# Layer 2 of a four-layer graph network: row maxima of unstacked scores on TensorE row blocks, a mask added in 32x32 blocks, and normalisation on GpSimd

## The chip, the cores and the metric

The kernel runs on one core of a Trainium2 chip. The metric is device time in microseconds (us), from the first to the last instruction and what the runtime adds around them. The kernel before takes 1164.12 us (median of three runs, 1162.89 to 1165.49).

## The reference

Four layers run one after the other over `x` (16 batches, 512 nodes, 128 features) with one 512x512 adjacency matrix `adj`; each ends in a residual and a layer norm. The change touches layer 2, masked attention with 4 heads of 32 features:

```python
qkv = h @ W                                   # (16, 512, 384)
q, k, v = ...                                 # each (16, 4 heads, 512, 32)
mask = jnp.where(adj == 0, -jnp.inf, 0.0)
scores = jnp.einsum('bhid,bhjd->bhij', q, k) / np.sqrt(HEAD_DIM) + mask
attn = jax.nn.softmax(scores, axis=-1)
out = jnp.einsum('bhij,bhjd->bhid', attn, v)
x = _layernorm(x + out, axis=-1)
```

Everything is float32 at the interface. The kernel keeps that precision by splitting operands into a high part that TensorE multiplies in one pass (float32r) and a low part that holds the rest.

## The kernel before, in words

`build` runs `layer0_setup`, `layer0`, `layer1`, `layer2` and `layer3` in turn; each has a block in which every engine has its own instruction list, tied together by semaphores. `x` stays in SBUF as `m.X`. `mask_ij` and `mask_ji` hold -1e30 where an edge is missing, with rows i or rows j on the partitions.

Layer 2 is a software pipeline over the 16 batches. In step s every engine runs through the list `ORDER`; the item `what` works on batch s - STAGE[what]. The helper `pairs` unrolls the first steps, loops over two steps at a time and unrolls the last ones. `Fori` is the hardware loop. A step of the full pipeline holds, for one batch each:

- `N T R B Y`: batch norm of layer 1 applied (ScalarE), turned (TensorE, L1282), added to the residual (VectorE, L1197), statistics (VectorE), 1/sqrt (GpSimd, L505 and L507), applied (VectorE, L513) and copied into `m.X` (GpSimd, L1117).
- `x q k v`: the batch is turned (L1287), split in two parts, and multiplied with the weights: q and k in three float32r passes (L58 to L60), v in float32 (L1299). q and k are split in two again as `qkT`.
- stacking: SyncE copies `qkT` by DMA into `qk_st` (L1088), so that one head has 96 rows: high, high, low of q against high, low, high of k. A product over 96 rows then has all three terms. Row 96 takes the negated row maximum of q's side against a row of ones.
- `s`, 16 of them (4 heads by 4 row tiles): one product of 96 rows (L1306) into a PSUM bank; VectorE adds `mask_ij` and takes the maximum along the row in one instruction (L1221, and a second that reads the accumulator).
- `g n`: the 16 maxima are negated, turned (L1310), copied out (L1164) and sent by DMA into row 96 (L1079).
- `t`, 8 of them (4 heads by 2 pairs of column tiles): the transposed scores (L1319) and `mask_ji` through an identity matrix (L1320), two banks (`wide`, 128x1024) each; ScalarE takes the exponential of both (L1160).
- `a`, 4 of them: output and denominator (L1331). Each is four matmuls that use 32 columns of the array each and fill 32 partitions of bank 4 or 5, over four steps of j. They are float32, which the trace shows as two records per matmul.
- `e o d m r b y`: copied out (L1168, L1170), turned back (L1338, L1343), divided (L1231, L1237), residual (L1243), layer norm (statistics on VectorE, L492 and L498; root on GpSimd; application on VectorE, L513).

Items in `RING` take banks 6 and 7 in turn, and before TensorE writes into one it waits for what the item before last released (`wait_for_bank`): for an `s` that is its maximum on VectorE. So two units of scores can be in flight.

Of the kernel before, what the change touches and what calls it, by code (L numbers as in the profile page):

```python
# [20 lines left out]
F32 = mybir.dt.float32  # L21
# [6 lines left out]
P = 128  # L28
B, N, D = 16, 512, 128
NT = N // P  # L30
# [36 lines left out]
def setup_constants(nc, ctx, m, ins, bank):  # L67
# [9 lines left out]
    m.mask_ji = sb("mask_ji", [P, NT, N], BF16)  # L77
    m.AhT = [sb("AhT_hi", [P, NT, N], F32R), sb("AhT_lo", [P, NT, N], F32R)]
# [888 lines left out]
def layer2(nc, m, ins, bank, wide):  # L967

    SCALE = float(HD) ** -0.5
    JP = NT // 2
    PAIRS = H * JP
    TILES = H * NT
    with ExitStack() as own:
# [3 lines left out]
        def sem(name):  # L992
# [7 lines left out]
        xTr = [[sb(f"xT{k}{h}", [P, N], F32R) for h in range(2)] for k in range(2)]  # L1000
        qkT = [sb(f"qkT{k}", [P, 4, N], F32R) for k in range(2)]
        Q_LO, Q_HI, K_HI, K_LO = range(4)
        qk_st = [sb(f"qk_st{k}", [P, 2, H, N], F32R) for k in range(2)]
        q_st = [s[:, 0] for s in qk_st]
        k_st = [s[:, 1] for s in qk_st]
        v = [sb(f"v{k}", [P, NT, D]) for k in range(2)]
        junk = [sb(f"junk{k}", [P, N], BF16) for k in range(2)]
        mx = [sb(f"mx{k}", [P, TILES]) for k in range(2)]
        neg = [sb(f"neg{k}", [P, TILES]) for k in range(2)]
        neg_row = [sb(f"neg_row{k}", [TILES, P], F32R) for k in range(2)]  # L1010
        prob = [[sb(f"prob{k}{h}", [P, 2, N]) for h in range(H)] for k in range(JP)]
# [9 lines left out]

        w_in = sem("w_in"); w_hi = sem("w_high"); w_lo = sem("w_low"); const = sem("const")
        x_f = sem("x_in_place")
# [4 lines left out]
        stacked = [[sem(f"stacked{k}{h}") for h in range(H)] for k in range(2)]  # L1028
        s_ps = sem("scores"); s_mx = sem("row_max")
        n_sb = sem("negated"); n_ps = sem("neg_turned"); n_row = sem("neg_row_out")  # L1030
        row_in = [sem(f"row_in{k}") for k in range(2)]
        t_ps = sem("scores_t"); t_exp = sem("exp_done")
        av = sem("values")
# [4 lines left out]
        psO, psD = bank[4], bank[5]  # L1038
# [10 lines left out]
        ORDER = []  # L1049
        for what in ("s s g Y a n s N R x T a B s q k a s e s a s s t s t s d t m o r s t t s v b t s s y t t s s").split():  # L1050
            ORDER.append((what, sum(w == what for w, _ in ORDER)))

        RING = [item for item in ORDER if item[0] in "Txqkvsnod"]
        ring = {item: bank[6 + n % 2] for n, item in enumerate(RING)}

        def released(s, what, k):

            b = s - STAGE[what]
            return {"x": (x_c, after(b, 1)), "q": (q_lo, after(b, 1)), "k": (k_lo, after(b, 1)),
                    "v": (v_c, after(b, 1)), "s": (s_mx, after(b, TILES, k + 1)),  # L1060
                    "n": (n_row, after(b, 1)), "o": (o_n, after(b, 1)),
                    "d": (rcp, after(b, 1)), "T": (res1, after(b, 1))}[what]

        def of_batch(what, s, par, nth):

            back = STAGE[what]
            return s - back, (par + back) % 2, nth + (par - back) // 2

        @block.sync
        def _(sp):  # L1070
            sp.dma_start(W[:], ins["L2_gnn_W"]).then_inc(w_in, 16)
            for k in range(2):
                sp.sem_inc(row_in[k], 16)

            def step(s, par, alive, nth):
                if alive[2]:
                    sp.wait_ge(n_row, after(s - 2, 1))
                    hold(sp, gate)
                    sp.dma_start(q_st[par][3 * HD:3 * HD + 1].bitcast(F32).rearrange("a h (t p) -> a (h t) p", p=P),  # L1079
                                 neg_row[par][:].bitcast(F32)).then_inc(row_in[par], 16)  # L1080
                if alive[0]:
                    sp.wait_ge(k_lo, after(s, 1))
                    for h in range(H):
                        sp.wait_ge(t_ps, after(s - 2, PAIRS, (h + 1) * JP))
                        if h == 0:
                            hold(sp, gate)
# [596 lines left out]
```

## Time and profile before

| | |
|---|---|
| median of 3 runs | 1164.12 us |
| the profiled execution, span | 1163.7 us |
| steps of layer 2 with all stages full | 12, from 592 to 914 us |
| layer 2 in all | from 500 to 983 us |
| TensorE busy over the span | 86% |
| VectorE, ScalarE, GpSimd busy | 63%, 39%, 17% |

The profile comes from one profiled execution, whose span is 1163.7 us; this lies 0.4 us under the median of the runs, so one can be read for the other. "Busy" of an engine is the union of its instruction records. Matmul records overlap, since each begins before the one ahead of it has left the array: what one costs in a stream is read from start to start. "PEld" is the loading of the stationary operand. In the names, `128*32` means that the stationary operand has 128 rows and 32 columns. "Granted clock" is a share of 2.4 GHz; 0.5 is 1.2 GHz.

### The profile page before, as it was taken

Reading aid. Unit: us, or ns where it says so; the run is one execution under the profiler, and the core shown is the slowest. Engines: PE = TensorE matmul, PEld = TensorE weight load, DVE = VectorE, ACT = ScalarE, POOL = GpSimd, SP = SyncE. Lnnn points to the kernel's source line nnn. Section 1 sums busy time; section 2 is a strip of 40 time slices with the busy share of each in tenths; the row PEclk is TensorE's granted clock in tenths of the full one; section 3 lists DMA queues with packets and bytes.
Section 4 is the critical chain, followed back from the end, with each engine's and each line's share of the span. In section 5 each row is a group of like instructions: output and inputs, shape, how many; then the busy total and the mean of one; then the engine's idle time right before and its main releaser. Section 6 shows DMA issues by size and latency. Waiting matters only on the chain. (4 is left out here: it accounts for less than half of the span.)

```text
span 1163.7 us, 19102 instructions
## 1 busy us (share of the span) xinstructions
PE 1002.3 (86%) x5486; PEld 681.5 (59%) x5532; DVE 727.6 (63%) x2226; ACT 450.3 (39%) x734; POOL 198.0 (17%) x266
## 2 busy tenths in 40 slices
PE   3969999999997697926899999999999995899995
PEld 2748999999997586413444444444444442566663
DVE  7853455554454565635667767777777642688885
ACT  2111121121120265710444444544544442577762
POOL 5000110111100000050011111111111001155554
PEclk7879999999998899955799999999999998899998
DMA  6000000000000000004222222222223200000001
GB/s 185 1 28 19 10 19 19 10 18 18 9 0 1 9 0 0 0 8 108 55 56 55 54 54 54 54 58 64 66 60 68 66 1 3 1 27 27 27 27 37
DMA packets 32629, 40.07 MB, mean 34 GB/s; under 512 B 6352, under 2 KB 15696, under 8 KB 32592
## 3 DMA queue, kind: packets, MB, share of 16 engines
q1 hardware_dynamic: 32592, 39.61, 13.9%
q8 instruction: 19, 0.31, 0.1%
q14 instruction: 18, 0.15, 0.0%
HBM read 5.91 MB, written 4.19 MB: 9 GB/s over the span
## 5 line engine op out<-in xcount | busy, mean ns | idle before, releaser
L1221 DVE CUSTOM_DVE_ANT_0 junk<-bank,mask_ij 128x512 bf16<-128x512 f32 x256 | 170.7, 689 | 80.7 <-PE bank L1306 75.6
L1160 ACT ACTIVATE prob<-wide 128x1024 f32<-128x1024 f32 x128 | 128.0, 1024 | 44.5 <-PE wide L1320 44.1
L1306 PE MATMUL bank<-qk_st 96*128 96x512 f32 x256 | 122.2, 517 | 25.3 <-DVE mx L1221 15.8
L1319 PE MATMUL wide<-qk_st 128*128 128x512 f32 x256 | 116.2, 523 | 0.3 <-ACT prob L1160 0.3
L596 ACT CAST yT<-wide 128x512 fp32r<-128x512 f32 x48 | 28.1, 586 | 217.6 <-PE wide L699 162.7
L505 POOL TENSOR_SCALAR n_rstd<-n_aggr 128x4 f32<-128x4 f32 x64 | 12.6, 198 | 506.7 <-DVE n_aggr L498 494.6
L1306 PEld LDWEIGHTS bank<-qk_st 96*128 96x128 f32 x256 | 49.2, 201 | 82.5 <-DVE mx L1221 37.4
L1320 PE MATMUL wide<-mask_ji,identb 128*128 128x512 bf16 x226 | 88.8, 393 | 0.0
L58 PE MATMUL bank<-z,L3T_hi 128*128 128x256 f32 x256 | 73.8, 288 | 6.3 <-DVE z L657 6.3
L1633 PEld LDWEIGHTS bank<-Wh,pr 128*128 128x128 f32 x512 | 61.1, 196 | 23.8 <-issue 19.9
L1633 PE MATMUL bank<-Wh,pr 128*128 128x129 f32 x512 | 65.3, 282 | 10.9 <-ACT pr L1501 10.9
L60 PE MATMUL bank<-z,L3T_lo 128*128 128x256 f32 x256 | 73.8, 288 | 0.0
L59 PE MATMUL bank<-z,L3T_hi 128*128 128x256 f32 x256 | 73.6, 288 | 0.0
L1331 PE MATMUL bank<-prob,v 128*32 128x512 f32 x512 | 68.1, 604 | 1.8 <-ACT prob L1160 1.8
L507 POOL TENSOR_TENSOR n_rstd<-n_rstd,neg_half 128x4 f32<-128x4 f32 x64 | 66.3, 1036 | 5.5 <-POOL n_rstd L505 0.2
L1331 PE MATMUL bank<-prob,ones_hd 128*32 128x512 f32 x512 | 66.6, 592 | 0.0
L643 DVE TENSOR_TENSOR yT<-wide,yT 128x512 fp32r<-128x512 f32 x48 | 32.9, 686 | 50.9 <-ACT yT L596 50.9
L1320 PEld LDWEIGHTS wide<-mask_ji,identb 128*128 128x128 bf16 x256 | 24.7, 96 | 62.3 <-issue 59.2
L58 PEld LDWEIGHTS bank<-z,L3T_hi 128*128 128x128 f32 x256 | 50.3, 196 | 7.6 <-DVE z L657 6.8
L1319 PEld LDWEIGHTS wide<-qk_st 128*128 128x128 f32 x256 | 50.5, 197 | 4.0 <-ACT prob L1160 1.3
L619 POOL TENSOR_TENSOR Xr<-Xf,Xr 128x512 fp32r<-128x512 f32 x16 | 20.3, 1288 | 185.1 <-ACT Xr L591 185.1
L513 POOL TENSOR_SCALAR rc<-rc,n_aggr,n_rstd 128x128 f32<-128x128 f32 x64 | 50.0, 794 | 3.4 <-POOL n_rstd L507 3.4
(256 smaller groups left out, 2273.3 us busy)
## 6 DMA issues: line engine op xcount, KB each, us to landing
qk_st<-qkT SPq DMA_DIRECT2D x192, 128.0 KB, 2.4
Xf<-X SPq DMA_DIRECT2D x16, 256.0 KB, 2.3
out_dram<-rc SPq DMA_DIRECT2D x16, 256.0 KB, 2.3
A<-in_adj_dram SPq DMA_DIRECT2D x1, 1024.0 KB, 5.5
w<-in_L_gnn_W_dram SPq DMA_DIRECT2D x2, 128.0 KB, 2.3
qk_st<-neg_row SPq DMA_DIRECT2D x16, 8.0 KB, 1.8
W<-in_L_gnn_W_dram SPq DMA_DIRECT2D x1, 192.0 KB, 2.4
w_sb<-in_L_gnn_w_dram SPq DMA_DIRECT2D x1, 64.0 KB, 5.0
```

The lines of the kernel that those rows point to most:

```text
L58: pe.matmul(out, stat[0], mov[0], start=start, stop=False)
L59: pe.matmul(out, stat[0], mov[1], start=False, stop=False)
L60: return pe.matmul(out, stat[1], mov[0], start=False, stop=stop)
L507: pool.tensor_tensor(rstd[:], rstd[:], self.m.neg_half[:, 0:4], ALU.pow).then_inc(self.s_rstd, 1)
L513: eng.tensor_scalar(out(k), r[:, k], self.aggr[parity][:, k, 0:1], self.rstd[parity][:, k:k + 1], ALU.subtract, ALU.mult).then_inc(self.s_ ...
L1160: act.activation(flat(prob[jp][h][:]), wide[k % 2][:], ACT.Exp, scale=SCALE).then_inc(t_exp, 1)
L1221: dve.tensor_tensor_reduce(out=junk[k % 2][:], in0=src[:], in1=m.mask_ij[:, k % NT], scale=1.0, scalar=3.0 * MASKED, op0=ALU.add, op1=ALU.max,
L1306: pe.matmul(out[:], q_st[bp][0:3 * HD, h, i * P:i * P + P], k_st[bp][0:3 * HD, h], start=True, stop=True).then_inc(s_ps, 1)
L1319: pe.matmul(ps, k_st[bp][:, h, j * P:j * P + P], q_st[bp][:, h], start=True, stop=False)
L1320: last = pe.matmul(ps, m.identb[:], m.mask_ji[:, j], start=False, stop=True)
L1331: last = pe.matmul(ps[c, :], v[bp][:, k, c] if stat is None else stat[:], prob[jp][h][:, jj], start=(k == 0), stop=(k == NT - 1), skip_gro ...
L1633: last = pe.matmul(out_bank[h][:, t * (D + 2):t * (D + 2) + D + 1], pr[par][:, j, k * P:k * P + P], Wh[par][:, j, 0:D + 1], start=(j == 0) ...
```

## The change

Only `layer2` is new, beside one remembered address and the declaration of the PSUM banks (a third pair, `wide[2]`, is banks 4 and 5).

1. `s` has 8 units in place of 16. A unit is one row tile of two heads: two matmuls of 32 rows each, on neighbouring row blocks of the array, of `qkT`'s high parts alone, into banks 4 and 5; then `mask_ij` through the identity into each bank. VectorE takes one plain maximum over 2x512. There is only this one pair of banks, so a unit waits for the maximum of the unit before.
2. `t` has 4 units, one head each, over banks 0 to 3: four matmuls of `qk_st`, then `mask_ji` in 16 matmuls of 32x32 (row block j, column block c), from a rearranged copy `mask_q`, which 16 DMAs fill once.
3. `a` becomes `D` (denominators) and `V` (outputs), each a complete accumulation over j in a bank of the ring; `prob` is double buffered (two of its eight parts lie where `AhT` of layer 1 was), and `qk_st` single.
4. The maxima are turned and sent in two halves (`n`, `m`), negated by ScalarE's copy.
5. GpSimd applies both norms, copies, subtracts for `xT`'s low part, and adds the residual. VectorE has none of these.
6. Stages: 6 deep in place of 5; every engine has an order of its own.

```diff
-        STAGE = dict(N=0, T=0, R=0, B=0, Y=1, x=1, q=1, k=1, v=2, s=2, g=3, n=3, t=3,
-                     a=4, e=4, o=4, d=4, m=4, r=4, b=4, y=4)
...
+        DEPTH = 6
+        STAGE = dict(N=0, T=0, R=0, B=1, x=1, q=1, k=1, v=2, s=2, n=2, m=3, t=3, E=3,
+                     D=4, V=4, e=4, f=4, d=4, o=4, c=4, b=5)
...
+        PE_ORDER = order("t s m D D s D D t s V V x s V V t s n s q d t o s k v T s")
+        ACT_ORDER = order("E E m e E E x f E E n q N E E k v")
+        DVE_ORDER = order("B s s s b s s s q c s k R s")
+        RING = [(what, k) for what, k in PE_ORDER if what in "TxqkvnmoVDd" and (what not in "VD" or k == 0)]
         ring = {item: bank[6 + n % 2] for n, item in enumerate(RING)}
...
+                if alive[1]:
+                    b, bp = s - 1, 1 - par
+                    norm1.root(pool, b + CREDIT, bp)
+                    norm1.apply(pool, b + CREDIT, bp, Xf[bp], lambda k: Xf[bp][:, k])
+                    pool.wait_ge(norm1.s_x, after(b, 4))
+                    hold(pool, gate)
+                    pool.tensor_copy(batch_flat(m.X, b), flat(Xf[bp][:])).then_inc(x_f, 1)
+                    pool.wait_ge(x_c, after(b, 1))
+                    pool.wait_ge(k_ps, after(b - 1, 1))
+                    pool.tensor_tensor(xTr[1][:], xT[bp][:], xTr[0][:].bitcast(F32),
+                                       ALU.subtract).then_inc(x_lo, 1)
+                if alive[5]:
+                    b, bp = s - 5, 1 - par
+                    norm.root(pool, b + CREDIT, bp)
+                    norm.apply(pool, b + CREDIT, bp, r, lambda k: r[:, k])
...
-                        dve.tensor_tensor_reduce(out=junk[k % 2][:], in0=src[:], in1=m.mask_ij[:, k % NT],
-                                                 scale=1.0, scalar=3.0 * MASKED, op0=ALU.add, op1=ALU.max,
-                                                 accum_out=mx[bp][:, k:k + 1]).then_inc(s_mx, 1)
...
+                        dve.tensor_reduce(mx[bp][:, col:col + NT + 1:NT], wide[2][:].rearrange("p (h n) -> p h n", h=2),
+                                          AX.X, ALU.max).then_inc(s_mx, 1)
...
-                        pe.matmul(out[:], q_st[bp][0:3 * HD, h, i * P:i * P + P], k_st[bp][0:3 * HD, h],
-                                  start=True, stop=True).then_inc(s_ps, 1)
...
+                        pe.wait_ge(s_mx, after(b, UNITS, k))
+                        for hh in range(2):
+                            c = slice((2 * pair + hh) * HD, (2 * pair + hh + 1) * HD)
+                            pe.matmul(bank[4 + hh][:], qkT[bp][c, Q_HI, i * P:i * P + P], qkT[bp][c, K_HI],
+                                      start=True, stop=False)
+                        for hh in range(2):
+                            last = pe.matmul(bank[4 + hh][:], m.identb[:], m.mask_ij[:, i], start=False, stop=True)
+                        last.then_inc(s_ps, 1)
...
-                            pe.matmul(ps, k_st[bp][:, h, j * P:j * P + P], q_st[bp][:, h], start=True, stop=False)
-                            last = pe.matmul(ps, m.identb[:], m.mask_ji[:, j], start=False, stop=True)
...
+                        for j in range(NT):
+                            if j % 2 == 0:
+                                pe.wait_ge(t_exp, after(b, EXPS, 2 * k - 1 + j // 2))
+                            pe.matmul(bank[j][:], k_st[:, k, j * P:j * P + P], q_st[:, k], start=True, stop=True)
+                        for c in range(4):
+                            for j in range(NT):
+                                q = slice(32 * j, 32 * j + 32)
+                                last = pe.matmul(bank[j][32 * c:32 * c + 32, :], m.identb[q, q], mask_q[q, c],
+                                                 start=False, stop=True, skip_group_check=True)
                         last.then_inc(t_ps, 1)
```

How the change moves instructions. On TensorE, in the full step before, the stretch from the last two `a` items on. `bank<-qk_st` is a unit of scores, `bank<-prob,v` and `bank<-prob,ones_hd` the two halves of an `a`, `wide<-qk_st` with `wide<-mask_ji,identb` the transposed scores:

```order
L1331 MATMUL bank<-prob,v 32x512 x4
L1331 MATMUL bank<-prob,ones_hd 32x512 x4
L1306 MATMUL bank<-qk_st 128x512 x2
L1331 MATMUL bank<-prob,v 32x512 x4
L1331 MATMUL bank<-prob,ones_hd 32x512 x4
...
L1306 MATMUL bank<-qk_st 128x512
...
L1306 MATMUL bank<-qk_st 128x512
...
L1319 MATMUL wide<-qk_st 128x512
L1320 MATMUL wide<-mask_ji,identb 128x512
L1319 MATMUL wide<-qk_st 128x512
L1320 MATMUL wide<-mask_ji,identb 128x512
```

The beginning of a full step of the change. `wide<-qk_st` with the 16 rows of `mask_q` is one `t`; `wide<-qkT` with `wide<-mask_ij` is one `s`; `ident,mx` is the turned maximum:

```order
L1340 MATMUL wide<-qk_st 128x512 x4
L1344 MATMUL wide<-mask_q,identb 32x512 x16
L1322 MATMUL wide<-qkT 128x512 x2
L1325 MATMUL wide<-mask_ij,identb 128x512 x2
L1282 MATMUL bank<-ident,mx 8x128
L1355 MATMUL bank<-prob,ones_hd 32x512 x8
L1322 MATMUL wide<-qkT 128x512 x2
L1325 MATMUL wide<-mask_ij,identb 128x512 x2
L1355 MATMUL bank<-prob,ones_hd 32x512 x8
L1340 MATMUL wide<-qk_st 128x512 x4
L1344 MATMUL wide<-mask_q,identb 32x512 x16
```

Each `s` and each `t` now has matmuls of two shapes, 32-row or 32x32 blocks beside whole ones, where before only the `a` items had blocks. Later in the same step, in the stretch from the third `t` on, two units of scores stand next to each other with only the turned maximum between them; the product of q and the turned denominators (`ident,denT`) follow:

```order
L1340 MATMUL wide<-qk_st 128x512 x4
L1344 MATMUL wide<-mask_q,identb 32x512 x16
L1322 MATMUL wide<-qkT 128x512 x2
L1325 MATMUL wide<-mask_ij,identb 128x512 x2
L1282 MATMUL bank<-ident,mx 8x128
L1322 MATMUL wide<-qkT 128x512 x2
L1325 MATMUL wide<-mask_ij,identb 128x512 x2
L58 MATMUL bank<-xT_hi,Wr 128x512
L59 MATMUL bank<-xT_lo,Wr 128x512
L60 MATMUL bank<-xT_hi,Wr 128x512
L1366 MATMUL bank<-ident,denT 128x128 x4
```

Before, the units of one step were spread between `a` items and in groups of two or three over two banks; here each has the one pair of banks to itself.

On GpSimd a full step before had two roots and one copy. Now, in the last unrolled step ahead of the loop (n1 is the norm of layer 1, n2 that of layer 2), it has:

```order
L506 TENSOR_SCALAR n_rstd<-n_aggr 128x4 [waits n1_aggr,n1_x]
L508 TENSOR_TENSOR n_rstd<-n_rstd,neg_half 128x4 [waits n1_eps]
L514 TENSOR_SCALAR Xb<-Xb,n_aggr,n_rstd 128x128 [waits n1_rstd]
L514 TENSOR_SCALAR Xb<-Xb,n_aggr,n_rstd 128x128 x3
L1116 COPY X<-Xb 128x512 [waits n1_x]
L1119 TENSOR_TENSOR xT_lo<-xT,xT_hi 128x512 [waits k_in_psum,xT_out]
L506 TENSOR_SCALAR n_rstd<-n_aggr 128x4 [waits n2_aggr,n2_x]
L508 TENSOR_TENSOR n_rstd<-n_rstd,neg_half 128x4 [waits n2_eps]
L514 TENSOR_SCALAR rb<-rb,n_aggr,n_rstd 128x128 [waits n2_rstd]
L514 TENSOR_SCALAR rb<-rb,n_aggr,n_rstd 128x128 x3
L1127 COPY X<-rb 128x512 [waits n2_x]
L1133 TENSOR_TENSOR rb<-rb,X 128x512 [waits out_divided,x_in_place]
```

The chain from the statistics to the turned batch (`x`) now passes through four GpSimd instructions where VectorE had them.

## Rows read from the trace of the kernel before

**Rows 1.** Timeline of ScalarE: start, length, instruction, idle before and releaser
```profile
591.99 0.59 ACT L1168 COPY oT<-bank 128x512 f32<-128x512 f32 x1 [3.81 <-PE bank L1331]
914.30 0.59 ACT L1168 COPY oT<-bank 128x512 f32<-128x512 f32 x1 [3.81 <-PE bank L1331]
```
**Rows 2.** Busy time by stretch: stretch, engines busy with counts, PEclk, DMA share, GB/s
```profile
619.04:914.30 295.26, 273.89 (x1548) 125.26 (x1571) 211.01 (x695) 141.40 (x187) 31.90 (x53) 1.00 0.27 59
500.20:591.99 91.79, 59.12 (x212) 30.05 (x214) 47.70 (x153) 22.40 (x33) 18.93 (x20) 0.65 0.24 54
```
**Rows 3.** Waits of TensorE from 619.04 to 914.30: total us, times, longest
```profile
PE bank L1306 <- DVE mx L1221: 10.0, 11, 1.0
```
**Rows 4.** Timeline of TensorE, pieces of one full step
```profile
731.13 0.60 PE L1338 MATMUL bank<-ident,oT 128*128 128x128 f32 x4
731.49 0.48 PE L1306 MATMUL bank<-qk_st 96*128 96x512 f32 x1
...
732.07 0.58 PE L1319 MATMUL wide<-qk_st 128*128 128x512 f32 x1
...
732.53 0.58 PE L1319 MATMUL wide<-qk_st 128*128 128x512 f32 x1
...
733.96 1.16 PE L1299 MATMUL bank<-W,xT 128*128 128x128 f32 x8
734.87 0.48 PE L1319 MATMUL wide<-qk_st 128*128 128x512 f32 x1
735.19 0.39 PE L1320 MATMUL wide<-mask_ji,identb 128*128 128x512 bf16 x1
...
749.06 0.40 PE L60 MATMUL bank<-xT,Wr 128*128 128x512 f32 x1
749.39 1.06 PE L1331 MATMUL bank<-prob,v 128*32 128x512 f32 x8
750.27 1.04 PE L1331 MATMUL bank<-prob,ones_hd 128*32 128x512 f32 x8
751.24 0.72 PE L1306 MATMUL bank<-qk_st 96*128 96x512 f32 x2
751.90 1.06 PE L1331 MATMUL bank<-prob,v 128*32 128x512 f32 x8
```
**Rows 5.** Timeline of TensorE in layer 3: whole float32 matmuls, two records each
```profile
1060.16 1.02 PE L1624 MATMUL wide<-xTc,wB 128*128 128x512 f32 x2
1061.01 1.02 PE L1627 MATMUL wide<-xTc,wB 128*128 128x512 f32 x2
```
**Rows 6.** One line alone, the plain reduction of 2048: min/median/max ns
```profile
L296 DVE TENSOR_REDUCE deg<-A x1: 2286/2286/2286, 34.6 to 34.6; 128x4 f32<-128x2048 f32 x1
```
**Rows 7.** Instruction groups, 619.04 to 914.30: count | busy us, mean ns | idle before
```profile
L1221 DVE CUSTOM_DVE_ANT_0 junk<-bank,mask_ij 128x512 bf16<-128x512 f32 x176 | 117.1, 689 | 47.7 <-PE bank L1306 44.6 <-DVE mx L1221 3.1
```
**Rows 8.** Timeline: VectorE releases TensorE, TensorE releases ScalarE
```profile
748.35 0.08 DVE L1221 DVE_READ_ACCUMULATOR2_ANT mx<- 128x1 f32 x1
748.49 0.50 PE L58 MATMUL bank<-xT,Wr 128*128 128x512 f32 x1 [0.67 <-DVE mx L1221]
...
755.03 0.39 PE L1320 MATMUL wide<-mask_ji,identb 128*128 128x512 bf16 x1
...
755.46 1.02 ACT L1160 ACTIVATE prob<-wide 128x1024 f32<-128x1024 f32 x1 [0.49 <-PE wide L1320]
```
**Rows 9.** Groups of GpSimd over the whole span, columns as in Rows 7
```profile
L507 POOL TENSOR_TENSOR n_rstd<-n_rstd,neg_half 128x4 f32<-128x4 f32 x64 | 66.3, 1036 | 5.5 <-POOL n_rstd L505 0.2
L513 POOL TENSOR_SCALAR rc<-rc,n_aggr,n_rstd 128x128 f32<-128x128 f32 x64 | 50.0, 794 | 3.4 <-POOL n_rstd L507 3.4
L619 POOL TENSOR_TENSOR Xr<-Xf,Xr 128x512 fp32r<-128x512 f32 x16 | 20.3, 1288 | 185.1 <-ACT Xr L591 185.1
```
**Rows 10.** Timeline of GpSimd, the start of layer 2
```profile
499.88 11.08 POOL L1102 MEMSET qk_st<- 32x2048 f32 x6
```
**Rows 11.** Timeline of VectorE, the end of layer 2
```profile
981.68 1.11 DVE L513 TENSOR_SCALAR X<-rb,n_aggr,n_rstd 128x128 f32<-128x128 f32 x4 [1.66 <-POOL n_rstd L507]
```

More of the change, by code:

```diff
@@ new lines, in neg, with stack @@
+            def neg(b, p):
+                sp.wait_ge(n_row[p], after(b, 1))
+                sp.wait_ge(t_ps, after(b - 1, H, 2 * p + 2))
+                hold(sp, gate)
+                sp.dma_start(q_st[3 * HD:3 * HD + 1, 2 * p:2 * p + 2].bitcast(F32).rearrange("a h (t p) -> a (h t) p", p=P),
+                             neg_row[p][:].bitcast(F32)).then_inc(row_in[p], 16)
+            def stack(b, bp, h):
+                sp.wait_ge(t_ps, after(b - 1, H, h + 1))
+                hold(sp, gate)
+                for g, (q, k) in enumerate(((Q_HI, K_HI), (Q_HI, K_LO), (Q_LO, K_HI))):
+                    sp.dma_start(qk_st[g * HD:(g + 1) * HD, :, h].bitcast(F32),
+                                 qkT[bp][h * HD:(h + 1) * HD, q:k + 1:k - q].bitcast(F32)).then_inc(stacked[h], 16)
@@ L1075, in step @@
             def step(s, par, alive, nth):
+                if alive[3]:
+                    neg(s - 3, 1)
                 if alive[2]:
[L1077 to L1086, printed above, removed]
-                        for g, (q, k) in enumerate(((Q_HI, K_HI), (Q_HI, K_LO), (Q_LO, K_HI))):
-                            sp.dma_start(qk_st[par][g * HD:(g + 1) * HD, :, h].bitcast(F32),
-                                         qkT[par][h * HD:(h + 1) * HD, q:k + 1:k - q].bitcast(F32)
-                                         ).then_inc(stacked[par][h], 16)
+                    b = s - 2
+                    sp.wait_ge(q_lo, after(b, 1))
+                    sp.wait_ge(k_lo, after(b, 1))
+                    stack(b, par, 0)
+                    stack(b, par, 1)
+                    neg(b, 0)
+                    stack(b, par, 2)
+                    stack(b, par, 3)
@@ L1127, in step @@
             def step(s, par, alive, nth):
-                for what, k in ORDER:
+                for what, k in ACT_ORDER:
                     if not alive[STAGE[what]]:
@@ L1166, in step @@
                         act.wait_ge(av, after(b, NT))
                         act.wait_ge(o_ps, after(b - 1, 1))
[L1168 to L1172 removed]
+                        act.copy(oT[:], ring["V", 0][:]).then_inc(o_c, 1)
+            pairs(act, B, DEPTH, step)
         @block.vector
         def _(dve):
[L1176 removed]
+            for s in (res1, q_lo, k_lo, rcp, o_n):
@@ new lines, in step @@
+                        for c in range(4):
+                            for j in range(NT):
+                                q = slice(32 * j, 32 * j + 32)
+                                last = pe.matmul(bank[j][32 * c:32 * c + 32, :], m.identb[q, q], mask_q[q, c],
+                                                 start=False, stop=True, skip_group_check=True)
+                        last.then_inc(t_ps, 1)
+                    elif what in "DV":
+                        acc = ring[what, 0]
+                        if what == "D" and k == 0:
+                            pe.wait_ge(t_exp, after(b, EXPS))
+                        if what == "V" and k == 0:
+                            pe.wait_ge(v_c, after(b, 1))
+                        for h in range(H):
+                            c = slice(h * HD, (h + 1) * HD)
+                            last = pe.matmul(acc[c, :], ones[:] if what == "D" else v[bp][:, k, c], prob[bp][h][:, k],
+                                             start=(k == 0), stop=(k == NT - 1), skip_group_check=True)
+                        last.then_inc(dn if what == "D" else av, 1)
```

260 lines of the change are left out of this document (122 added, 138 removed).

## The prediction

> **What bounds the kernel now.** I read how long a step is first, then the busy time by stretch, the waits and the timeline of TensorE. In the twelve full steps of layer 2, which run from 591.99 to 914.30 us by ScalarE's copy of the output, one per step [rows 1], a step takes (914.30 - 591.99) / 12 = 26.86 us. Over eleven of them TensorE is busy 273.89 of 295.26 us, VectorE 211.01, ScalarE 141.40, GpSimd 31.90, at the full clock [rows 2]. So TensorE sets the step: idle (295.26 - 273.89) / 11 = 1.94 us per step. Of that, 10.0 / 11 = 0.9 us is a unit of scores that waits for the maximum two before it on VectorE [rows 3]. VectorE has 211 / 11 = 19.2 us of work and is late only there.
>
> From start to start on the timeline of TensorE [rows 4]: a pair `t` matmul and mask matmul 732.53 - 732.07 = 0.46 us, so 0.23 for one full matmul; a half of an `a` 0.88. A step before is then
>
> - `s`: 16 x 0.23 = 3.7
> - `t`: 16 x 0.46 = 7.4
> - `a`: 4 x 1.96 = 7.8 (0.88, then 0.97 with the way out, then 0.11 more in what follows, below)
> - idle 1.9
> - what is left of 26.86: 6.0, for q, k, v, five turnings and small gaps. This part stays.
>
> **The change on TensorE.** Three prices aren't in the trace as such.
>
> *Change of shape.* The `a` items use 32-column blocks and stand between whole matmuls. L60 to L1331 takes 749.39 - 749.06 = 0.33 in place of 0.23; the second half of the `a` takes 751.24 - 750.27 = 0.97 in place of 0.88; and the two L1306 behind it take 0.66 in place of 0.46, which holds the 0.11 of the way out and 0.10 of the next way in [rows 4]. A way in and out is thus 0.10 + 0.09 + 0.11 = 0.30 us. Not all of it is the shape: the matmul behind v's product, which has no blocks, also takes 735.19 - 734.87 = 0.32. So the shape itself costs 0.2. The bounds for the round trip in a new item are 0 (everything hidden) and 0.30; I take 0.20. The Trainium skill ("TensorEngine Tiling (Array Packing)", Key Properties) says that a change of tiling mode drains TensorE. The trace agrees with that for column blocks, by 0.2 to 0.3 us; for row blocks no row here shows it. That rule speaks against this change, which makes 12 such round trips more in each step. By a drain of nothing the sum would be about 2 us less per step.
>
> *Two row blocks at once.* The two 32-row matmuls of an `s` cost 0.23 if they run side by side, 0.46 if not. The nearest row is the `a`: its half has four float32 matmuls (eight records) in 0.88 us [rows 4], and one whole float32 matmul of 512 columns in layer 3 takes 1061.01 - 1060.16 = 0.85 [rows 5]: four column blocks run at once. I take 0.23 for the pair. An `s` is then 0.23 + 2 masks x 0.23 + 0.20 = 0.89, and 8 x 0.89 = 7.1.
>
> *Sixteen 32x32 blocks.* All at once 0.23, four at once as the `a` does 4 x 0.23 = 0.92. I take 0.25, since rows and columns of blocks are separate here and banks too. `t` is 4 x 0.23 + 0.25 + 0.20 = 1.37, and 4 x 1.37 = 5.5. The Trainium skill ("TensorE: Matmul & The Clock Gate", Measured speedup vs the span model) gives 10.6 times for sixteen such tiles. By that the mask would be 0.23 x 16 / 10.6 = 0.35 us, an estimate from the page, and the step 0.4 us longer.
>
> `D` and `V` have as many matmuls as `a`: 7.8. At four places (`D s`, and `t s` three times) one block shape follows another, so a way is saved: -0.4. One more turned maximum: +0.2.
>
> **The new waits on TensorE.** An `s` waits for the maximum of the `s` ahead. The plain maximum over 2x512 is half of 2286 ns, 1.15 us [rows 6], as against two of 0.69 [rows 7]. From VectorE's end (748.35 + 0.08) to TensorE is 0.06; from the slot of the last matmul (755.03 + 0.23) to the reader is 0.20 [rows 8]. So `s` to `s` needs 0.20 + 1.15 + 0.06 = 1.4 us of other work between them. Six of the eight gaps have 1.8 us or more. Between the fifth and sixth there is only the turned maximum, 0.15: a wait of 1.3 us. Behind it on TensorE are q, d and the fourth `t`, and all that is left of the step.
>
> The second wait is `T`, in the bank of k. The low part of k on VectorE comes after k's copy on ScalarE, which stands behind the two exponentials of the fourth `t`: 0.20 + 2 x 1.02 + 0.59 + 0.69 (ScalarE and VectorE as in [rows 1, 7, 8]) and some 0.1 of handing over are 3.6 us after that `t`. TensorE has o, `s`, k and v meanwhile: 0.36 + 0.89 + 3 x 0.23 + 0.91 [rows 4] = 2.85. So 0.8 us. I see no third one above 0.1: idle 1.3 + 0.8 + 0.1 = 2.2.
>
> Sum of a step: 7.1 + 5.5 + 7.8 - 0.4 + 0.2 + 6.0 + 2.2 = 28.4 us, 1.55 more than 26.86. What TensorE is spared in `t` (1.9) it more than pays in `s` (3.4), since the mask left VectorE for it.
>
> **The other engines** don't set the step. VectorE: 8 x 1.15 for 16 x 0.69, and about 4.4 us of norm application, residual and subtraction gone: near 15 us. GpSimd: two roots 2 x 1.3, two applications 2 x 4 x 0.79, a subtraction and an addition 2 x 1.29 [rows 9], copies 1.2: 12.7 us in 28. Its chain from the statistics to `x` is 1.4 + 1.3 + 3.2 = 6 us from the start of the step, and TensorE comes to `x` at 11. These edits cost nothing while that is so; without the 5 us of cover a slower GpSimd would go one to one into the step. The DMAs: `qk_st` is single, but a head's stack is copied as soon as its `t` is done and is wanted a step later; the copy takes some 2 us. The maxima of heads 0 and 1 leave at 18 us of the step and are wanted at its end. The 16 DMAs for the mask are issued before the first `t` by over 50 us.
>
> **Start and end.** The six memsets of 11.08 us hold up the first statistics and root [rows 10]; three are left: -5.5. At the end a residual on GpSimd (1.3 for 0.7), the application (3.2 for 1.1 [rows 11]), and a copy (0.6): +3.3. Together -2. The steps that fill and drain (91.8 us ahead of the first full one, at 0.65 of the clock [rows 2]) have the same items; I count four of them, half each, so 14 steps: 14 x 1.55 = 22.
>
> 1163.7 + 22 - 2 = 1183.7 us; the median shown is 0.4 above the profiled span, so **1184**.
>
> **Rivals.**
>
> 1. *Faster.* The change of shape costs nothing where the next stationary operand can be loaded meanwhile: 8 x 0.2 + 4 x 0.2 - 0.4 = 2.0 less, 26.4 per step: 1163.7 - 14 x 0.46 - 2 = 1155. If the waits also fall into gaps that I count under the 6.0, it reaches 1125. For it: VectorE is relieved by 4 us, and the waits of before (0.9 and others) go. Against it: the 0.30 around each `a`, and the fixed 1.3.
> 2. *Slower, the blocks don't run at once.* Row blocks one after another: 8 x 0.23 = 1.8 more per step, 1184 + 14 x 1.8 = 1209. If the mask also goes four by four, 0.67 x 4 = 2.7 more, 1247. Against: the `a`. For: there the blocks are columns only. This is also the case in which the change doesn't do what it says.
> 3. *Slower, TensorE is bound by issue.* The densest stretch in the rows is an `a`: 16 instructions, loads included, in 0.88 us, 55 ns each. If that were a limit, 32 instructions for a mask take 1.76 in place of 0.25: 6.0 more per step, 1268. It decides as soon as the queue is used up; 1.76 us of mask behind 8 instructions of `t` would do that. The same 0.88 is explained by the columns alone, so the trace doesn't tell. The Trainium skill ("TensorE: Matmul & The Clock Gate", Wait — 56ns, not 53.3ns?) names about 62 ns per matmul where instructions are decoded in software, and about 25 where not.
>
> **How the numbers follow.** Forecast 0.42 (its own range 1168 to 1206, from the round trip between 0.15 and 0.30 and the mask up to 0.5); rival 1 0.36; rival 2 0.14; rival 3 0.08. The 0.36 is high because three terms that I added (change of shape, both waits) are worked out, not seen, and all on the same side. The range is 1128 to 1235: it leaves out the far ends of rivals 1 and 2 and all of rival 3. A measurement here tells 0.2% (2.3 us) from nothing: faster 0.36, same 0.05, slower 0.59.
>
> **What would show it.** A step of 28.4 us between ScalarE's copies; `s` about 0.89 from the first matmul to what follows, `t` 1.4; a wait of TensorE of 1.3 us per step for the maximum, ahead of the sixth `s`, and one of 0.8 ahead of L1295; VectorE near 15 us per step; GpSimd near 12.7 and not waited for. The prediction is wrong in its size if the two row matmuls start 0.23 apart, if the sixteen start over more than 0.5 us, and in its sign if whole matmuls follow blocks 0.23 later.

## The result, and the profile after

| | before | after |
|---|---|---|
| median | 1164.59 us (1162.89 to 1165.49) | 1169.34 us (1168.72 to 1169.67) |
| profiled span | 1163.7 | 1166.9 |
| forecast | | 1184 (1128 to 1235) |

The change is slower by 0.44%: ratio 1.0044, interval 1.0029 to 1.0058. The side was the one forecast, the size was not: +4.8 us where I had +20.

First the length of a step. From one reciprocal of the denominators on VectorE to the next it is 26.93 us before (mean of eleven) and 27.44 after: +0.51, where 1.55 was forecast. The busy times of the twelve-step stretch (columns: stretch, PE, PEld, DVE, ACT, POOL, PEclk, DMA share, GB/s) are, after,

```profile
592.00:907.00 315.00, 288.81 (x2360) 131.76 (x2393) 173.40 (x336) 146.01 (x206) 142.92 (x183) 1.00 0.26 59
```

VectorE has 173.40 x 27.44 / 315 = 15.1 us per step (19.2 before [rows 2]), GpSimd 12.5. Both were forecast (15 and 12.7). TensorE still sets the step, at the full clock. Its waits from 620 to 900 us, in the order total, times, longest:

```profile
PE wide L1322 <- DVE mx L1239: 12.1, 10, 1.2
PE bank L1295 <- DVE qkT L1231: 6.4, 11, 0.6
PE wide L1325 <- issue: 4.9, 31, 0.2
```

The wait of [rows 3] is gone, and the first two stand where the prediction put them: 1.21 us ahead of the sixth unit of scores (forecast 1.3), 0.58 ahead of L1295 (forecast 0.8). The third line is gaps of 0.16 us inside a unit, between its pair and its mask; they are counted as part of `s` below. The timeline of TensorE after, in pieces:

```profile
706.32 0.65 PE L1295 MATMUL bank<-ident,on 128*128 128x128 f32 x4 [0.58 <-DVE qkT L1231]
706.90 0.50 PE L1322 MATMUL wide<-qkT 32*128 32x512 f32 x2
707.34 0.61 PE L1325 MATMUL wide<-mask_ij,identb 128*128 128x512 bf16 x2
707.59 1.28 PE L1340 MATMUL wide<-qk_st 128*128 128x512 f32 x4
708.80 0.43 PE L1344 MATMUL wide<-mask_q,identb 32*32 32x512 bf16 x16
709.26 0.50 PE L1322 MATMUL wide<-qkT 32*128 32x512 f32 x2
...
725.11 0.27 PE L1282 MATMUL bank<-ident,mx 128*8 128x128 f32 x1
726.59 0.50 PE L1322 MATMUL wide<-qkT 32*128 32x512 f32 x2 [1.21 <-DVE mx L1239]
```

These answer to [rows 4]. Read the starts. The pair of row blocks has 707.34 - 706.90 = 0.44 us until the next item: 0.23 for two at once and 0.21 for the way out of the shape. Four `t` matmuls have 708.80 - 707.59 = 1.21, and the sixteen blocks 709.26 - 708.80 = 0.46 (0.36 in the step's other three). The sixteen start within 0.05 us of one another. So all sixteen run beside each other, and the two row blocks too; `e4` to `e6` below test both. The other rows:

```profile
L1239 DVE TENSOR_REDUCE mx<-wide 128x2 f32<-128x1024 f32 x128 | 156.8, 1225 | 163.2 <-PE wide L1325 162.1
L508 POOL TENSOR_TENSOR n_rstd<-n_rstd,neg_half 128x4 f32<-128x4 f32 x64 | 67.0, 1046 | 5.5 <-POOL n_rstd L506 0.2
```

The plain maximum of 2x512 takes 1.23 us (1.15 forecast from [rows 6]), in place of two of 0.69 [rows 7]. The root is as in [rows 9]. In the full steps no wait of TensorE names GpSimd.

At the ends, the memsets fell from 11.08 us [rows 10] to 5.55, and the first root starts at 509.56 in place of 512.69. The last item of layer 2 ends at 986.58, before at 982.79. These 3.8 us are the sum of four parts: the first reciprocal comes 3.7 earlier, the eleven full steps take 5.6 more, the last four between reciprocals 1.7 less, and from the last reciprocal to the end it is 3.6 more.

### The profile page after: what moved, and what is told of

It is laid out like the page before. It is cut to its first block and busy times, and to the rows that moved or that the text cites. A ratio compares the mean times of both kernels' runs of the same rounds, so it can differ in the third digit from the quotient of the medians.

```text
span 1166.9 us, 20377 instructions
## 1 busy us (share of the span) xinstructions
PE 999.8 (86%) x6510; PEld 678.1 (58%) x6572; DVE 657.4 (56%) x1666; ACT 447.9 (38%) x750; POOL 345.3 (30%) x439
## 5 line engine op out<-in xcount | busy, mean ns | idle before, releaser
L1239 DVE TENSOR_REDUCE mx<-wide 128x2 f32<-128x1024 f32 x128 | 156.8, 1225 | 163.2 <-PE wide L1325 162.1
L1322 PE MATMUL wide<-qkT 32*128 32x512 f32 x256 | 66.1, 511 | 26.8 <-DVE mx L1239 25.9
L1340 PE MATMUL wide<-qk_st 128*128 128x512 f32 x256 | 78.5, 428 | 0.8 <-ACT prob L1182 0.7
L1325 PE MATMUL wide<-mask_ij,identb 128*128 128x512 bf16 x210 | 70.3, 400 | 7.5 <-issue 7.5
L652 DVE TENSOR_TENSOR G<-wide,bias_field 128x384 f32<-128x384 f32 x64 | 35.7, 558 | 71.0 <-PE wide L60 71.0
L58 PE MATMUL wide<-Pj_hi,yT 128*128 128x384 f32 x192 | 64.5, 336 | 2.8 <-DVE yT L644 2.8
L1322 PEld LDWEIGHTS wide<-qkT 32*128 32x128 f32 x256 | 24.5, 187 | 69.6 <-DVE mx L1239 53.7
L60 PE MATMUL wide<-Pj_hi,yT 128*128 128x384 f32 x192 | 64.3, 335 | 0.0
L59 PE MATMUL wide<-Pj_lo,yT 128*128 128x384 f32 x192 | 64.3, 335 | 0.0
L514 POOL TENSOR_SCALAR rb<-rb,n_aggr,n_rstd 128x128 f32<-128x128 f32 x64 | 50.3, 799 | 3.4 <-POOL n_rstd L508 3.4
L514 POOL TENSOR_SCALAR Xb<-Xb,n_aggr,n_rstd 128x128 f32<-128x128 f32 x64 | 50.3, 798 | 3.4 <-POOL n_rstd L508 3.4
```

Of the source, the lines that this page charges most:

```text
L58: pe.matmul(out, stat[0], mov[0], start=start, stop=False)
L59: pe.matmul(out, stat[0], mov[1], start=False, stop=False)
L60: return pe.matmul(out, stat[1], mov[0], start=False, stop=stop)
L514: eng.tensor_scalar(out(k), r[:, k], self.aggr[parity][:, k, 0:1], self.rstd[parity][:, k:k + 1], ALU.subtract, ALU.mult).then_inc(self.s_ ...
L1239: dve.tensor_reduce(mx[bp][:, col:col + NT + 1:NT], wide[2][:].rearrange("p (h n) -> p h n", h=2), AX.X, ALU.max).then_inc(s_mx, 1)
L1322: pe.matmul(bank[4 + hh][:], qkT[bp][c, Q_HI, i * P:i * P + P], qkT[bp][c, K_HI], start=True, stop=False)
```

## The experiments

Each is timed in turn with the kernel before on the same chip; ratios are to it, with a 95% interval. "Step" is the mean of eleven steps from reciprocal to reciprocal. Ledgers of a step are differences of starts on TensorE's timeline, waits taken out. Where the clock fell in some steps, the length of the others is given as "step at clock 1.00".

### The two waits

Theory: they cost what they last, since TensorE sets the step. `e1` moves the second half's items between the two units of scores, `e2` puts `T` behind the last unit, `e3` does both.

```diff
-        PE_ORDER = order("... V V t s n s q d t o s k v T s")
+        PE_ORDER = order("... V V t s n q d s t o s k v s T")   # e1: "n q d s", e2: "s T"
-        DVE_ORDER = order("B s s s b s s s q c s k R s")
+        DVE_ORDER = order("B s s s b s s q s c s k s R")             # e1: "q s c", e2: "s R"
```

> The changed kernel with q and the turned denominators put between the fifth and sixth unit of scores (TensorE: 's n q d s t o'; VectorE: 's q s c'). Theory A, the step is TensorE's list of work plus the waits seen on it: the wait of 1.21 us ahead of the sixth unit goes, since n, q and d take 0.27 + 0.88 + 0.36 = 1.5 us; a step 26.25 in place of 27.46, over some 14 steps -17 us, about 1152. Rival B, the wait only moves: q's low part on VectorE now comes later or the turned output waits for its bank, and the time stays within 4 us of 1169.

> The changed kernel with the turning of the next batch (T) behind the last unit of scores of the step, on TensorE ('k v s T') and VectorE ('k s R'). Theory A: the wait of 0.58 us for k's low part is covered by the unit of scores, -0.6 per step, -8 us, about 1161. Rival B: the residual R now comes right ahead of the next step's statistics and the turned maximum waits for T's bank, so the wait moves into the next step and the time stays within 3 us of 1169.

> Both moves together. Theory A: the two gains add, 25.65 us per step and about 1144 (-25). Rival B: with TensorE's idle time gone VectorE or the exponentials of ScalarE are late somewhere; more than a third of the sum is lost, over 1152.

Measured: e1 1159.35 us, 0.9965 [0.9951, 0.9978], step 26.85. e2 1160.93, 0.9971 [0.9961, 0.998], step 27.09. e3 1146.78, 0.9859 [0.9839, 0.9879], step 26.01. e1 missed by 7 us, and its waits (620 to 900 us) tell why:

```profile
PE bank L1295 <- DVE qkT L1231: 6.4, 11, 0.6
PE wide L1325 <- issue: 4.9, 31, 0.2
PE bank L1366 <- ACT neg_row L1146: 4.6, 10, 0.5
```

The wait of 1.21 is gone, and 0.47 of it comes back in the third line: `d` now comes earlier, and its bank is that of the turned maximum, whose copy stands behind two exponentials on ScalarE. At the full clock the two gains nearly add up: a step is 26.85 in e1 (-0.59), 26.53 in e2 (-0.91, more than the 0.58 of its wait) and 26.01 in e3 (-1.43). In time they don't: 10.0 and 8.4 us against 22.6 for both. The clock fell in several steps of e2 and not in those of e1 and e3 (more on this below), so that e2's mean step is 27.09. Two placements are thus worth 22.6 us, five times what the change costs, and either alone is enough to make it faster than the kernel before.

### The prices of the new shapes

`e5` puts both heads' matmuls on one row block, so that they can't run at once. `e6` reads all 128 rows in them, so no shape changes, and none run at once. `e4` adds the mask of `t` with four whole matmuls. `e12` is that edit on e3's order. e5 and e6 compute other scores than the reference.

```diff
-                            c = slice((2 * pair + hh) * HD, (2 * pair + hh + 1) * HD)
+                            c = slice(2 * pair * HD, (2 * pair + 1) * HD)      # e5
+                            c = slice(0, P)                                    # e6
...
-                        for c in range(4):
-                            for j in range(NT):
-                                q = slice(32 * j, 32 * j + 32)
-                                last = pe.matmul(bank[j][32 * c:32 * c + 32, :], m.identb[q, q], mask_q[q, c], ...)
+                        for j in range(NT):                                    # e4, e12
+                            last = pe.matmul(bank[j][:], m.identb[:], m.mask_ji[:, j], ...)
```

> The changed kernel with both 32-row matmuls of a unit of scores on the same row block (the same head twice, so the row maximum of the odd heads is that of their neighbour; everything else as it is). Theory A: what was one slot of 0.23 becomes two, +0.22 per unit, +1.8 per step, +25 us, about 1194: that is what running on two row blocks at once is worth. Rival B: they didn't run at once before (the modelled ends hide it), no change.

> The changed kernel with both matmuls of a unit over all 128 rows (the row maxima are then of the sum over the four heads; everything else as it is). No change of shape is left in a unit, and nothing runs at once: 4 x 0.22 = 0.88 us. Theory A, a change of shape in and out costs 0.2 beside the pair's 0.23: against 0.88 for a unit now, no difference per unit, within 4 us of 1169, and about 25 us under the run with one row block. Rival B, the shape costs nothing: as slow as the run with one row block.

> The changed kernel with the mask of the transposed scores added as in the kernel before: four whole matmuls with the identity per head in place of sixteen 32x32 ones. Theory A, the sixteen run at once: the trace has 0.36 us for them from their first to the next item, four whole ones take 4 x 0.22 = 0.88, so +0.45 per head less a change of shape (0.1), +1.3 to +1.8 per step, 1187 to 1195. Rival B, the sixteen with their sixteen loads cost as much as whole ones once the ways in and out are counted: within 3 us of 1169.

> The order of e3_both (1146.8 us, 26.0 us per step, longest wait 0.6 us) with t's mask as four whole matmuls instead of sixteen blocks. At full clock that edit cost 1.8 us per step in e4_mask_whole; there the steps in which TensorE's granted clock fell behind the 1.21 us wait of the sixth unit of scores were 3.5 us longer. Theory A (the fall belongs to that wait): here the wait is gone, the clock stays at 1.00, a step takes 27.8 us and the kernel 1146.8 + 14 x 1.8 = 1172 us (1168 to 1175). Theory B (the fall comes with the whole-mask matmuls whatever waits stand before them): the mean step is 28.5 or more, the clock of the layer is 0.97 or below, and the time is 1180 us or more.

| | median | ratio | step at clock 1.00 | step mean |
|---|---|---|---|---|
| e5 | 1214.7 | 1.0424 [1.0398, 1.045] | 29.3 | 30.70 |
| e6 | 1174.83 | 1.0091 [1.0074, 1.0108] | 28.0 | 28.01 |
| e4 | 1203.44 | 1.0327 [1.0311, 1.0342] | 29.25 | 29.97 |
| e12 | 1176.17 | 1.0094 [1.0077, 1.0111] | 27.8 | 27.86 |

At the full clock the prices can be read from the step. e5: +1.86 = 8 x 0.23, so a second matmul on the same row block costs its whole 0.23. e6: +0.57 = 8 x 0.07, where I had expected nothing; side by side saves 0.23 of a unit and pays 0.16 of it for the change of shape (the 1.3 us between e5 and e6 are 8 x 0.16). e4: +1.8 = 4 x 0.45, and e12 the same against e3 (27.86 - 26.01 = 1.85): at 0.92 for four whole matmuls (4 x 0.23), the sixteen blocks cost 0.92 - 0.46 = 0.46 with their change of shape. I had 0.25 + 0.20. The Trainium skill ("TensorEngine Tiling (Array Packing)", Key Properties) says that a change of mode drains TensorE; the 0.16 here agrees.

In time, e4 missed by 8 us and e5 by 21 (e6 by 2, e12 by 1). For e4 and e5 the granted clock shows where (e5, same columns as above):

```profile
714.00:716.00 2.00, 1.30 (x5) 0.42 (x5) 0.77 (x1) 1.89 (x3) 2.00 (x4) 1.00 0.00 0
716.00:718.00 2.00, 1.49 (x5) 0.63 (x5) 0.46 (x1) 0.18 (x2) 1.34 (x2) 0.71 0.01 2
718.00:720.00 2.00, 2.00 (x7) 1.51 (x7) 1.23 (x1) 0.20 (x1) 0.00 (x0) 0.50 0.70 159
720.00:722.00 2.00, 2.00 (x26) 1.32 (x25) 0.85 (x2) 1.22 (x3) 0.00 (x0) 0.94 0.19 38
...
811.00:840.00 29.00, 26.70 (x206) 12.16 (x208) 15.04 (x29) 12.75 (x18) 12.28 (x16) 1.00 0.24 55
```

```profile
715.03 0.27 PE L1282 MATMUL bank<-ident,mx 128*8 128x128 f32 x1
716.51 0.95 PE L1322 MATMUL wide<-qkT 32*128 32x512 f32 x2 [1.21 <-DVE mx L1239]
717.39 1.03 PE L1325 MATMUL wide<-mask_ij,identb 128*128 128x512 bf16 x2
717.86 0.99 PE L58 MATMUL bank<-xT_hi,Wr 128*128 128x512 f32 x1
718.65 0.63 PE L59 MATMUL bank<-xT_lo,Wr 128*128 128x512 f32 x1
719.08 0.63 PE L60 MATMUL bank<-xT_hi,Wr 128*128 128x512 f32 x1
719.50 0.97 PE L1366 MATMUL bank<-ident,denT 128*128 128x128 f32 x4
```

Behind the wait of 1.21 us the clock is 0.50 (the lower of the two levels, 1.2 GHz) for some 3 us, and a whole matmul has 719.50 - 719.08 = 0.42 instead of 0.23. In another step of the same run it stays at 1.00 (last row of the first fence). e12 tests whether the wait has to do with it. In the stretch from 592 to 907 e4 has the mean clock 0.97, and e12, with the same matmuls and a longest wait of 0.4 us, 1.00:

```profile
592.00:907.00 315.00, 305.35 (x1779) 138.67 (x1815) 172.13 (x333) 144.06 (x205) 139.54 (x179) 1.00 0.26 57
```

So the whole masks don't bring the fall by themselves. The long wait is not enough for it either, since e6 has the same one at 1.00 throughout the stretch.

### What the row mask costs

`e7` leaves the mask out of the row maxima; `e8` brings both norm applications back to VectorE (stages and orders, credits moved with them).

```diff
-                        for hh in range(2):                                    # e7
-                            last = pe.matmul(bank[4 + hh][:], m.identb[:], m.mask_ij[:, i], start=False, stop=True)
...
-        DVE_ORDER = order("B s s s b s s s q c s k R s")                       # e8
+        DVE_ORDER = order("B s s Y s b s s s q y c s k R s")
```

> The changed kernel without the two mask matmuls of a unit (the row maximum is then taken over all columns, masked ones too; the mask of the transposed scores stays). Theory A: the mask on TensorE costs 2 x 0.22 and the way out of the row shape moves into the next item, so 8 x 0.44 = 3.5 us per step; the waits for the maximum stay at 1.4 between units: the one wait grows by nothing, and a step is 27.46 - 3.5 = 24.0, 1169 - 14 x 3.5 = 1120. Rival B: VectorE's maximum then sets the pace and the gain is under half, over 1145.

> The changed kernel with both norm applications back on VectorE (as Y and y; the roots, copies, subtraction and residual stay on GpSimd). VectorE gets 2 x 1.1 us more per step. Theory A: VectorE isn't on TensorE's way while it is under 20 us in 27, and the instructions lie in its idle time: within 3 us of 1169. Rival B: every VectorE instruction ahead of a maximum delays a unit of scores, since there is one pair of banks only: +1.1 or +2.2 per step, 1184 to 1200.

e7: 1116.87 us, 0.9589 [0.9573, 0.9605], step 24.17 (24.05 but for one step). The mask costs 27.44 - 24.05 = 3.4 us of a step, 8 x 0.42, and 52.5 us in all. That is more than the whole difference of the two kernels. e8: 1172.64, 1.0077 [1.006, 1.0095], +3.3 us, just over the 3 expected; the clock is 0.98 in its mean and a new wait of 0.2 us shows in five steps. The move of the norms to GpSimd is thus worth 3.3 us at most by itself, and part of that is the clock.

### A better version

`e9` adds the row mask in 64x64 blocks, four per bank pair, as `t` does with 32x32; `e10` is e9 on e3's order; `e11` adds one move on ScalarE, against the wait that e1 brought up. Not shown: `mask_x`, a copy of the mask with its halves exchanged, which two DMAs fill once, and the two `neg_row`, which lie in one tensor.

```diff
-                        for hh in range(2):
-                            last = pe.matmul(bank[4 + hh][:], m.identb[:], m.mask_ij[:, i], start=False, stop=True)
+                        for c in range(2):
+                            for hh in range(2):
+                                q = slice(64 * hh, 64 * hh + 64)
+                                last = pe.matmul(bank[4 + hh][64 * c:64 * c + 64, :], m.identb[q, q],
+                                                 (m.mask_ij if c == hh else mask_x)[q, i], ...)
...
-        ACT_ORDER = order("E E m e E E x f E E n q N E E k v")
+        ACT_ORDER = order("E E m e E E x f E n E q N E E k v")                 # e11
```

> The changed kernel, in which the mask of a unit of scores is added in four 64x64 blocks (rows 0 to 63 for the even head's bank, 64 to 127 for the odd one's) from the mask and a copy with its halves exchanged, in place of two whole matmuls. Theory A, blocks of different rows and banks run at once, as the run with one row block showed for 32 rows: 0.22 in place of 0.44, less 0.1 for a third change of shape: -0.1 to -0.2 per unit, -1 to -1.6 per step, -14 to -22 us, 1147 to 1155. Rival B, each change of shape costs 0.1 to 0.2 with its load, and the third takes all of it back: within 4 us of 1169.

> Both moves of the order together with the mask of the scores in 64x64 blocks. Theory A: what the blocks gain alone comes on top of 1147, so 1125 to 1133. Rival B: with TensorE some 24.5 us per step the maxima on VectorE come between the units again, and at most a third of it is seen, over 1140.

> e10_all with one more move: ScalarE sends the copy of the turned maximum (n) ahead of the second exponential of its group. In e10_all and e3_both the denominator's matmuls (L1366) wait 0.47 us per step on that copy. My theory: the wait is on the path of TensorE's turn, so a step loses 0.4 to 0.5 us: 25.28 to about 24.85, 14 steps, 1138.3 - 6 = 1132 us (1130 to 1134). Rival: the wait only moves on to the next user of a bank behind it (q's copy, or the sums that wait for the exponential that is now late by the copy), and the time stays at 1137 to 1139.

e9: 1166.2 us, 1.001 [0.9999, 1.0021], step 27.34, 11 us above what was expected: its clock is 0.97 in the stretch, and each of its falls follows the wait of 1.1 us. e10: 1138.27, 0.9782 [0.9767, 0.9796], step 25.28 = 26.01 - 0.73, so 0.09 per unit, at the full clock; that is less than the 0.1 to 0.2 expected, and the time is 5 us above its range. e11: 1130.43, 0.9687 [0.9664, 0.9709], step 24.58, at the fast end of what was expected. TensorE has one wait left in the stretch, of 0.4 us:

```profile
592.00:907.00 315.00, 314.47 (x2870) 141.09 (x2869) 188.34 (x365) 161.91 (x227) 155.52 (x200) 1.00 0.29 64
```

e11 is 3.1% faster than the kernel before and 38.9 us faster than the change.

### The term that failed: a unit of scores before

The forecast gave 3.7 us of a step before to the 16 units of scores, 0.23 each. By starts they took 6.05, 0.38 each. Such a unit has 96 rows among matmuls of 128. `e13` gives it 128 rows, `e14` gives `t` 96, `e15` issues it twice, `e16` cuts it to 64 columns (all on the kernel before; the lines of e14 and e15 are not shown).

```diff
-  pe.matmul(out[:], q_st[bp][0:3 * HD, h, i * P:i * P + P], k_st[bp][0:3 * HD, h], ...)
+  pe.matmul(out[:], q_st[bp][:, h, i * P:i * P + P], k_st[bp][:, h], ...)                       # e13
+  pe.matmul(out[:, 0:64], q_st[bp][0:3 * HD, h, i * P:i * P + P], k_st[bp][0:3 * HD, h, 0:64])  # e16
```

> The kernel before with its 16 units of scores reading all 128 rows of the stack in place of 96 (the added rows hold zeros, a one and an old shift, so the maxima that they give are other numbers). Theory A: a unit takes 0.38 us and not 0.23 because its 96-row shape stands among 128-row matmuls. Then those that do not stand beside an a item (ten of 16) come down to 0.23 and the step is 1.5 to 2.4 us shorter where the wait for VectorE does not take it: 24.6 to 25.5 us, 1126 to 1141 us. Theory B: the extra does not hang on the rows: a step stays at 26.9 and the time at 1164 within 2.

> The kernel before with the 16 transposed-score matmuls on 96 rows, which leaves the subtraction of the maximum out of the exponential; their masks stay on 128 rows. Theory A (a 96-row matmul among 128-row ones pays for the change of shape): every one of the 16 now stands between masks of 128 rows and costs 0.1 to 0.2 more, the step 28.5 to 30 us, 1190 to 1215 us. Theory B (it does not hang on the rows): no change, 1164 within 2.

> The kernel before with the matmul of each unit of scores issued twice (the second overwrites the first). Theory A: a matmul costs 0.23 and the other 0.15 of a unit's 0.38 are fixed, so 16 x 0.23 = 3.7 more per step, less up to 0.9 where waits for the maximum absorb it: 29.7 to 30.6 us, 16 batches: 1209 to 1223 us. Theory B: each such matmul costs 0.38: 6.1 more per step, 33 us, 1250 us or more.

> The kernel before with the matmul of each unit of scores on 64 of its 512 columns (the maxima are then taken over 448 columns of old contents). Theory A: 448 of 512 columns are 0.20 us, so a step is 16 x 0.20 = 3.2 shorter at most, 23.7 us, and the waits for VectorE's maxima take back up to 1.5 of it: 23.7 to 25.2, 1113 to 1137 us; 0.15 per unit stay. Theory B: the unit's whole 0.38 follows the columns: 0.33 x 16 = 5.3 shorter before waits, 21.6 to 23.5 us, 1078 to 1110 us.

e13: 1164.29, 1.0003 [0.9993, 1.0012]; e14: 1164.31, 1.0 [0.9991, 1.001]. The rows are not it. e15: 1205.53, 1.0355 [1.0337, 1.0372], step 29.47, +2.54, 3.5 us under the range of its theory A and far from B. The waits in its steps fell meanwhile (620 to 900 us; the longest was 1.0 and is 0.6):

```profile
PE bank L1307 <- DVE mx L1221: 5.0, 9, 0.6
PE bank L58 <- DVE mx L1221: 3.3, 9, 0.5
PE bank L1282 <- DVE mx L1221: 3.3, 9, 0.4
```

They sum to (5.0 + 3.3 + 3.3) / 9 = 1.3 us per step; before it was 1.9. So 16 matmuls added 2.54 + 0.6 = 3.1 us, 0.20 each, near the 0.23. A matmul is not dearer there; by starts, some 0.15 lies around each unit. The timeline of the kernel before shows three places of it:

```profile
738.02 0.81 PE L1306 MATMUL bank<-qk_st 96*128 96x512 f32 x2
739.80 1.04 PE L1306 MATMUL bank<-qk_st 96*128 96x512 f32 x2 [0.97 <-DVE mx L1221]
740.76 0.64 PE L1331 MATMUL bank<-prob,v 128*32 128x512 f32 x4
```

Two units behind `t`'s mask take 0.81 us until the wait (0.46 by my price), the next two 0.96, up to the blocks of an `a`. Part of the first 0.81 belongs to the mask ahead, whose start is followed at once by theirs: `t` has 6.79 us by starts where 16 x 0.46 are 7.4. How large that part is, e4 and e12 tell without starts: with whole masks a step has 1.81 to 1.85 us more, so `t` before is worth the 6.12 of after plus that, 7.95. Then 1.15 of the 2.35 us are time of `t`, and 1.2 stay with s, 0.08 per unit. This is an estimate, since e4's four masks stand behind their four matmuls and not between them. Of the 1.2, the prediction had counted 4 x 0.11 = 0.44 under `a`, as what follows it. e16 decides nothing: its median is 1153.0, above both theories, its runs lie between 1142.41 and 1160.1 us (0.9874 [0.9816, 0.9932]), and its clock is 0.94 over the stretch.

## Why the prediction was right or wrong

One step on TensorE, in us. The first two columns of numbers are the prediction's, the others are read from one step's timeline each (731.13 to 758.12 before, 702.53 to 729.99 after).

| | forecast before | forecast after | before | after |
|---|---|---|---|---|
| `s` | 3.7 | 7.1 | 6.05 | 6.73 |
| `t` | 7.4 | 5.5 | 6.79 | 6.12 |
| `a`, or `D` and `V` | 7.8 | 7.4 (with the -0.4) | 7.41 | 7.43 |
| the rest | 6.0 | 6.2 | 4.81 | 5.39 |
| waits | 1.9 | 2.2 | 1.93 | 1.79 |
| sum | 26.86 | 28.4 | 26.99 | 27.46 |

- **The step that failed** is in the first list: "`s`: 16 x 0.23 = 3.7", and with it "what is left of 26.86: 6.0 [...] This part stays." The 16 units took 6.05 by starts, and some 4.9 when `t` gets back the 1.15 that e4 and e12 show to be its own. What their price lacked was in the 6.0, and I let it stay although it went with the units. The sum of before was right, since the last term was its difference; the split wasn't. So s rose by 0.7 (by starts) or 1.8 (by that estimate), and not by 3.4; of the 1.6 that are missing, 1.2 are the price before and 0.4 that of after (6.73 for 7.1). The group that could have told me is [rows 4]: two L1306 take 0.66 there, and I gave the surplus to the shape change alone.
- **`t`** looks like the opposite error, a gain of 1.9 forecast and 0.7 by starts. It is mostly where a mask's time is booked: e4 and e12 measure the gain of the blocks as 1.81 and 1.85, so this term was right. Taken together, which leaves the booking out, s and t rose from 12.84 to 12.85, forecast from 11.1 to 12.6. That is the 1.5 that the forecast has too much.
- **The remainder** was not constant either. It was 4.81 and became 5.39: of the 0.6, 0.4 are the turned maxima, two in place of one, for which I had 0.2. For the waits I had +0.3, and they are 0.14 less. D and V took their 7.4; before, `a` has 7.41 by starts where I had 7.8, since the 0.44 behind it are booked on what follows. That the waits (0.4 too much) and the remainder (0.4 too little) cancel is luck; the step was forecast 0.96 too long.
- **The prices of the new shapes** held: pair side by side (e5), change of shape 0.16 for 0.20 (e6), sixteen blocks with it 0.46 for 0.45 (e4, e12). Rival 2 is excluded by e5 and e4, rival 3 by the sixteen in 0.36 to 0.46 us. Rival 1 had 26.4 for a step, and the 27.44 lie midway. Of its two reasons the first (shape changes hidden) is false, the second (waits fall into gaps under the 6.0) comes near the error, though it was time of the units and not the waits that was under it.
- **The waits** were right in place, and 1.21 and 0.58 for 1.3 and 0.8. e1 to e3 show that both are on the path, and the side of the result hangs on them: without either, the change is faster than the kernel before. The side was thus forecast for a reason that holds, but with the step 0.96 too long it had far less margin than it seemed.
- **VectorE and GpSimd** as forecast in their busy time; e8 shows that the norms on VectorE cost 3.3 us at most.
- **Fourteen steps and the ends** were near enough. With the measured step the forecast's own sum is 14 x 0.51 - 2 = 5.1 us, measured 4.8. Of the 15 us between forecast and result, 14 x (28.4 - 27.44) = 13.4 are the step. An edit that scales with the work has more: e12 against e3 is 29.4 / 1.85 = 16 steps, one for each batch. For the change that would be 16 x 0.51 = 8.2 us; its shorter filling and draining take back more of it than its longer end adds.

Open is what the 0.08 us (0.15 by starts) around a unit of scores consist of. They don't hang on its rows; e15 shows them not to double with the matmul. Open too is why the clock falls behind the same wait in one step and not in another; the change itself had it at 1.00 in all its full steps with that wait, in the one execution that was profiled.

## What to carry to other kernels

Cost what a change removes from the starts of those very instructions, item by item, and treat a remainder as a suspect, not as a constant: whatever the removed items' price lacks sits in it. Starts can book one item's time on the next, so check a price by an experiment that changes that item alone and read the length of the step. On the engine that sets the time, look for a placement of the items before judging a rebuilt stage, since here three moves in the orders and a mask in blocks turned +0.4% into -3.1%.

## What the runs showed of the hardware

- Sixteen 32x32 matmuls of 512 bf16 columns, on all row and column blocks, start within 0.05 us and take 0.36 to 0.46 us from their first start to the next item's (the change); four whole ones that do the same take 0.87 to 0.97 (e12).
- Two 32-row matmuls of 512 columns on neighbouring row blocks cost 0.23 us less than on the same one (e5); the change of shape in and out costs 0.16 per pair (e5 against e6).
- TensorE's clock can fall to 0.50 for about 3 us (once in e5 for 6.8) in a step that is otherwise busy. Every such fall in the full steps begins within 1.6 us after the end of a wait of 0.9 to 1.2 us: in some of the steps of e2, e4, e5, e8 and e9 (mean clock 0.95 to 0.98 from 592 to 907 us), in one of e7, and in every one of e16 (0.94), where the wait is 0.9 to 1.0. The wait is not enough for it: the change and e6 have the same 1.2 and the kernel before 1.0, without a fall in their full steps. No kernel whose longest wait was 0.6 us (e1, e3, e10, e11, e12, e15) showed it there. It costs 1.6 us per step in e5 (30.9 for 29.3), more than the wait.
